# A kernel of conv, attention and experts on one core: no loops, and a rebuilt opening

## The chip, the cores and the metric

The kernel runs on one core of a Trainium2 chip. The metric is the device time in microseconds (us) of one execution. The kernel before took 2601.42 us (median of 3 runs, 2597.09 to 2603.22). One more execution was taken by the hardware profiler: 2608.5 us, with a span of 2606.6 us from its first to its last instruction.

## The reference

The input `x` has 32 images of 56 x 56 x 32 in float32. Three blocks follow one another, each with a residual:

- Group norm (a statistic for each image and channel), batch norm over all images, signs, and a 3 x 3 convolution with binarized weights.
- Layer norm, then linear attention in 16 heads of 32. Keys and queries are `elu + 1`, weighted by a cosine and a sine of the position. Key-value sums are taken over all 3136 tokens of an image. The division, the value projection and the dense projection follow.
- Layer norm, a router over 8 experts, the best two of each token, and their weighted sum.

The batch norm needs the mean and the variance of all 32 images before the first image can be binarized. So the whole of `x` is read twice: once for the statistics, once for the work.

## The kernel before

**Opening.** SyncE issues all DMAs. `x` comes in eight chunks of four images (1568 KB each) into two staging buffers `stage[0]` and `stage[1]`. TensorE transposes each image in 7 tiles (L509). VectorE takes `bn_stats` of the two PSUM banks (L861) and releases them. A chunk may be loaded into a staging buffer when TensorE has turned the chunk before it there (`stage_turned`). SyncE issues the eye matrix, five small constants (L430), chunks 0 and 1 (L435), then twenty weights and tables (L446), and only then, in a loop, chunks 2 to 7 (L450). After them it issues the loads of image 0 (L462). TensorE's and VectorE's parts of the opening are loops too. VectorE's loop covers the first 24 images. Then it waits for all 25 constants, makes the constants of the convolution (L871 to L883), the float16 halves of the weights wq, wk and we (L887 to L889) and the selector `sel16` (L890), and measures the last eight images. It then aggregates 32 images (L894), and exchanges two small matmuls with TensorE (L518, L520) for the mean and the variance.

**The value fold.** Behind that, VectorE writes one head's value weights four times side by side (L909), TensorE multiplies them with the dense weights (L524), and this is done for 16 heads with two buffers in turn. ScalarE copies the result into `p2` (L667). GpSimd raises 32 variances to the power -0.5 (L770) and then one more number (L772). VectorE makes the scale and the threshold of the binarization (L918 to L926). Then the main part begins (first instruction L539).

**Main part.** A list `ORDER`, written out by hand, gives every step of an image a time within a period of 14, for each engine. `iteration(engine, i)` sorts the steps of the images in flight. Iterations go from -3 to 34. `walk` emits iterations -3 to 2 one after the other, then 3 to 28 in a loop that has two of them in its body (13 passes, 12 jumps back on each engine), then 29 to 34 one after the other. In the loop, waits and addresses are computed from the counter by registers.

Steps that are named below: XT (L539, transposes of an image), XC (L553, a centring matmul, the first of it is the mark by which an image is timed here), K and Q (L567, L592), R and RP (L618, the spread of the denominators), PN1 (GpSimd's L778, the first of its work in the main part).

Of the kernel before, what the change touches and what calls it, by code (L numbers as in the profile page):

```python
# [9 lines left out]
ALU = mybir.AluOpType  # L10
# [7 lines left out]
TILES = 7  # L18
# [171 lines left out]
LOOP_FIRST, LOOP_LAST = 3, B - 4  # L190


# [26 lines left out]
def walk(eng, name, step):  # L219

    tables = [rounds(RING, RING_SLOTS), rounds(MISC, 1)]

    def lookup(kind, m, n, t):
        if kind not in RING and kind not in MISC:
            return None
        table = tables[kind in MISC]
        n = n // 4 if kind == "DN" else n
        slot, no, before = table[kind, m, n]
        if t is not None:
            (_, no2, before2), last = table[kind, m + 2, n], LOOP_LAST - LOOP_FIRST - 1  # L230
            slot_z, no_z, before_z = table[kind, m + last, n]
            assert no_z == no + (no2 - no) * (last // 2) and slot_z == slot
            assert before_z == (before[0], before[1] + last, before[2])
            no = t * (no2 - no) + no
        if before is not None:
            before = (before[0], Img(t, before[1]), before[2])
        return slot, no, before

    def run(i, t=None):
        for kind, m, n in iteration(name, i):  # L240
            step(kind, Img(t, m), n, lookup(kind, m, n, t))

    for i in ITERATIONS:
        if i < LOOP_FIRST:
            run(i)
    with eng.Fori(0, (LOOP_LAST + 1 - LOOP_FIRST) // 2) as t:
        run(LOOP_FIRST, t)
        run(LOOP_FIRST + 1, t)
    for i in ITERATIONS:
        if i > LOOP_LAST:  # L250
            run(i)


def build(nc, x, gamma, beta, conv_taps, conv_rows, wq, wk, wv, wd, wd_b, we, eyec, eyem, mean4, pair, dsum, sel,
          p2c, tabdc, tabnc, tabkc, firstc, validc, out):
    ctx = ExitStack()
    with ctx:
# [80 lines left out]
        wvr = xres[0:32, 0:128]  # L338
# [16 lines left out]
        consts_in = sem("consts_in")  # L355
        eye_in = sem("eye_in")
# [69 lines left out]
        def _(sp):  # L426
            sp.dma_start(eye_center[:, :], eyec).then_inc(eye_in, 16)
            for dst, src in ((mean4_sb[:, :], mean4), (views["rows"], conv_rows),
                             (small[:, 0:1], gamma), (small[:, 1:2], beta), (small[:, 2:3], wd_b)):
                sp.dma_start(dst, src).then_inc(consts_in, 16)  # L430
            x4 = x.rearrange("(q b) h w c -> q b (h w c)", b=4).rearrange("q b (p f) -> q p b f", p=PT)

            def stage_load(q, k, turned):
                wait(sp, stage_turned, turned)
                sp.dma_start(stage[k], q).then_inc(stage_in[k], 16)  # L435

            for k in range(2):
                stage_load(x4[k], k, 0)
            for dst, src in ((pair_sb[:, :], pair), (eye_mean[:, :], eyem), (dsum_sb[:, :], dsum), (views["taps"], conv_taps),
                             (views["valid"], validc), (views["wqa"], wq[0]), (wqb_s, wq[1]), (views["wka"], wk[0]),  # L440
                             (wkb_s, wk[1]), (views["wea"], we[0]), (web_s, we[1]), (wva_s, wv[0]), (wvb_s, wv[1]),
                             (wd_s, wd), (p2[:, :, :, :, :].rearrange("p a b c d -> p (a b c d)"), p2c),
                             (tabd[:, :, :].rearrange("p a b -> p (a b)"), tabdc), (tabk[:, :, :].rearrange("p a b -> p (a b)"), tabkc),
                             (first[:, :], firstc), (views["sel"], sel),
                             (tabn[:, :, :].rearrange("p a b -> p (a b)"), tabnc)):
                sp.dma_start(dst, src).then_inc(consts_in, 16)  # L446
            with sp.Fori(1, 4) as t:
                for k in range(2):
                    wait(sp, stage_turned, t * 8 + (4 * k - 4))
                    sp.dma_start(stage[k], x4[bass.ds(t * 2 + k, 1)].rearrange("q p b f -> (q p) b f"))\  # L450
                        .then_inc(stage_in[k], 16)
# [44 lines left out]
        def _(pe):  # L496
# [3 lines left out]
            def turn(t):  # L500
                for k in range(2):
                    pe.wait_ge(stage_in[k], t * 16 + 16)
                    for b in range(4):

                        wait(pe, stage_read, t * 8 + (4 * k + b - 3))
                        for j in range(TILES):
                            bank = 2 * b + (j >= 4)
                            dst = ps[:, bank, (j % 4) * PT:(j % 4 + 1) * PT]
                            mm = pe.transpose(dst, stage[k][:, b, j * 128:(j + 1) * 128], eye[0:PT, 0:PT])  # L509
                        mm.then_inc(stage_turned, 1)  # L510

            turn(0)
            with pe.Fori(1, 4) as t:
                turn(t)

            pe.wait_ge(consts_in, 16 * 25)
# [4 lines left out]

            for h in range(HEADS):
                pe.wait_ge(dve_pre, 3 + h)
                mm = pe.matmul(ps[:, 2, C * h:C * h + C], wvr[:, :] if h % 2 == 0 else xres[0:32, 128:256],  # L524
                               wd_s[:, C * h:C * h + C], start=True, stop=True)
                mm.then_inc(pe_pre, 1)

            def step(kind, m, n, rd):
# [34 lines left out]
                elif kind == "K":  # L563
                    pe.wait_ge(z_in[0], m.at(256, 256))
                    for k in range(2):
# [90 lines left out]
            pe.wait_ge(dve_pre, 22)  # L656
# [4 lines left out]
        def _(act):  # L661
            act.wait_ge(dve_pre, 19)
# [7 lines left out]
            act.wait_ge(dve_pre, 22)  # L670
# [95 lines left out]
        def _(pool):  # L766
            nc.gpsimd.memset(power[:, :], -0.5).then_inc(pool_pre, 1)
            pool.wait_ge(pool_pre, 1)
            pool.wait_ge(dve_pre, 20)
            nc.gpsimd.tensor_tensor(bw[:, 4, :], bw[:, 3, :], power[:, :], ALU.pow).then_inc(pool_pre, 1)  # L770
            pool.wait_ge(dve_pre, 21)
            nc.gpsimd.tensor_tensor(bn_inv, bn_half, power[:, 0:1], ALU.pow).then_inc(pool_pre, 1)  # L772

# [63 lines left out]
        def _(dve):  # L837
# [17 lines left out]
            def measure(t):  # L855
                for k in range(2):
                    for b in range(4):
                        img = t * 8 + (4 * k + b)
                        dve.wait_ge(stage_turned, img + 1)
                        for h in range(2):  # L860
                            last = v.bn_stats(stats[:, bass.ds(img, 1), 6 * h:6 * h + 6].rearrange("p a k -> p (a k)"),  # L861
                                              ps[:, 2 * b + h, 0:HALF[h] * PT])
                        last.then_inc(stage_read, 1)

            with dve.Fori(0, 3) as t:
                measure(t)

            dve.wait_ge(consts_in, 16 * 25)
# [12 lines left out]
            link(v.tensor_scalar(tmp, views["taps"], 0.0, 2.0, ALU.is_ge, ALU.mult))  # L881
            link(v.tensor_scalar(tmp, tmp, -1.0, None, ALU.add))
            link(v.tensor_tensor(conv_w[:, :, :].rearrange("p a b -> p (a b)"), tmp, views["valid"], ALU.mult))  # L883

            for dst, a, b, w in ((wq16, views["wqa"], wqb_s, DH), (wk16, views["wka"], wkb_s, DH),
                                 (we16, views["wea"], web_s, 264)):
                link(v.tensor_tensor(a, a, b, ALU.subtract))  # L887
                link(v.tensor_copy(dst[:, 0:w], a))
# [231 lines left out]
```

## Time and profile before

| what | value |
|---|---|
| median of 3 runs | 2601.42 us |
| profiled execution, its time | 2608.5 us |
| its span | 2606.6 us |
| TensorE matmul busy | 2302.2 us, 88% |
| VectorE busy | 2190.3 us, 84% |
| GpSimd busy | 1733.6 us, 67% |
| ScalarE busy | 1559.9 us, 60% |
| mean granted TensorE clock | 0.954 |
| first instruction of the main part | 105.4 us |

Busy time is the time in which an engine executes. The granted clock is the share of 2.4 GHz that TensorE was given; 0.50 is 1.2 GHz. The chain of waits is the work that ended last, followed back from the end. "issue" as the cause of an idle time means that the engine waited for nothing that the profile shows.

### The profile page before, as it was taken

How to read it: one execution, taken by the hardware profiler on the slowest of the kernel's cores; microseconds unless marked ns; L12 is line 12 of the kernel's file. 1: busy time of each engine (PE TensorE's matmuls, PEld its weight loads, DVE VectorE, ACT ScalarE, POOL GpSimd, SP SyncE). 2: the span in 40 equal slices, each digit the busy share in tenths (PEclk: the TensorE clock that was granted, in tenths of full speed). 3: DMA queues.
4: the chain of work that ended last, by engine and by line, in shares of the span. 5: the costliest groups of instructions: out<-in, count | busy, mean ns of one | idle time of the engine just before them, and what ended most of it. 6: DMA issues, size and time to landing. Idle time of an engine off the chain costs nothing.

```text
span 2606.6 us, 51821 instructions
## 1 busy us (share of the span) xinstructions
PE 2302.2 (88%) x15908; PEld 1110.7 (43%) x15908; DVE 2190.3 (84%) x2976; ACT 1559.9 (60%) x2757; POOL 1733.6 (67%) x1415
## 2 busy tenths in 40 slices
PE   3458999999999999999999999999999999999962
PEld 3313444444444434444443444444443444444431
DVE  3447899899898989899898989889898989999962
ACT  0046766567666666576666666666666657666620
POOL 0123477777776777777677767767676777777675
PEclk7579999999999999999999999999999999999985
DMA  8211112122221211122211111222111122211001
GB/s 249 49 28 24 33 33 38 32 42 42 42 42 33 34 31 35 36 42 41 42 34 30 34 33 39 42 42 42 31 35 31 34 38 42 41 35 32 20 19 25
DMA packets 284893, 105.84 MB, mean 41 GB/s; under 512 B 246032, under 2 KB 279680, under 8 KB 284512
## 3 DMA queue, kind: packets, MB, share of 16 engines
q1 hardware_dynamic: 284640, 102.41, 19.9%
q8 instruction: 166, 2.72, 0.5%
q14 instruction: 87, 0.71, 0.1%
HBM read 31.19 MB, written 12.85 MB: 17 GB/s over the span
## 4 chain that ended last, share of the span: by engine, by line
PE 57%; DVE 21%; issue 11%; POOL 3%; ACT 3%; DMA 2%; SPq 2%; DVEq 0%; ACTq 0%; POOLq 0%
PE ps L576 11%; PE ps L627 9%; PE ps L567 6%; PE ps L601 6%; DVE qbuf L981 6%; PE ps L618 5%; PE ps L592 4%; DVE kbuf L975 4%; PE ps L652 3%; DVE rs L998 2%; PE ps L553 2%; PE ps L646 2%; PE ps L560 2%; PE ps L640 2%; DMA qbuf<-in_x 2%
## 5 line engine op out<-in xcount | busy, mean ns | idle before, releaser
L701 ACT ACTIVATE ebuf<-ps,small 112x1024 f32<-112x1024 f32 x448 | 499.4, 1115 | 357.4 <-PE ps L567 306.4
L795 POOL TENSOR_TENSOR qbuf<-spread_r,qbuf 128x896 f32<-128x896 f32 x224 | 468.6, 2092 | 354.5 <-ACT spread_r L736 354.5
L975 DVE SCALAR_TENSOR_TENSOR kbuf<-ps,ebuf 112x1024 f32<-112x1024 f32 x448 | 544.3, 1215 | 106.6 <-ACT ebuf L701 103.0
L706 ACT ACTIVATE ebuf<-ps,small 128x896 f32<-128x896 f32 x448 | 451.8, 1009 | 206.4 <-PE ps L592 150.5
L981 DVE SCALAR_TENSOR_TENSOR qbuf<-ps,ebuf 128x896 f32<-128x896 f32 x448 | 485.5, 1084 | 15.8 <-ACT ebuf L706 14.6
L576 PE MATMUL ps<-kbuf,xcs 112*64 112x512 f32 x1792 | 482.9, 617 | 6.8 <-DVE kbuf L975 6.2
L627 PE MATMUL ps<-qbuf,gmat 128*64 128x224 f32 x3584 | 387.2, 358 | 2.9 <-DVE pbuf L1009 2.9
L778 POOL TENSOR_TENSOR rstd<-varr,power 112x28 f32<-112x28 f32 x64 | 307.3, 4802 | 80.9 <-DVE varr L960 77.4
L567 PE MATMUL ps<-wk,z 128*112 128x512 f16 x896 | 287.7, 404 | 61.0 <-DVE qbuf L981 33.6
L824 POOL TENSOR_TENSOR prod<-prod 112x512 f32<-112x512 f32 x224 | 285.5, 1275 | 54.7 <-DVE prod L1065 54.7
L627 PEld LDWEIGHTS ps<-qbuf,gmat 128*64 128x64 f32 x3584 | 240.2, 136 | 155.7 <-issue 81.9
L1065 DVE TENSOR_TENSOR prod<-ps,gate 112x1024 f32<-112x1024 f32 x224 | 272.8, 1220 | 34.8 <-PE ps L652 19.2
L618 PE MATMUL ps<-rs,sel 128*128 128x448 f16 x896 | 248.0, 360 | 53.7 <-issue 36.1
L1003 DVE TENSOR_TENSOR qbuf<-ps,qbuf 128x896 f32<-128x896 f32 x224 | 243.2, 1086 | 33.9 <-PE ps L618 31.4
L592 PE MATMUL ps<-z,wq 128*128 128x448 f16 x896 | 245.8, 356 | 14.4 <-ACT spread_r L736 6.2
L736 ACT ACTIVATE spread_r<-ps 128x896 f32<-128x896 f32 x224 | 204.6, 913 | 64.3 <-PE ps L618 35.7
L601 PE MATMUL ps<-qbuf,dmat 128*32 128x448 f32 x1792 | 237.1, 569 | 1.1 <-DVE pbuf L1009 1.1
L567 PEld LDWEIGHTS ps<-wk,z 128*112 128x112 f16 x896 | 90.3, 131 | 267.4 <-issue 99.7
L827 POOL TENSOR_TENSOR prod<-prod 112x256 f32<-112x256 f32 x224 | 163.4, 729 | 17.6
L652 PE MATMUL ps<-we,z 128*112 128x256 f16 x896 | 148.0, 291 | 22.3 <-DVE prod L1065 10.2
L618 PEld LDWEIGHTS ps<-rs,sel 128*128 128x128 f16 x896 | 63.0, 101 | 233.1 <-issue 138.5
L576 PEld LDWEIGHTS ps<-kbuf,xcs 112*64 112x64 f32 x1792 | 96.3, 136 | 148.9 <-issue 96.2
(131 smaller groups left out, 3090.7 us busy)
## 6 DMA issues: line engine op xcount, KB each, us to landing
z<-zhl SPq DMA_DIRECT2D x1024, 49.0 KB, 1.9
qbuf<-in_x SPq DMA_DIRECT2D x8, 1568.0 KB, 12.2
xt<-in_x SPq DMA_DIRECT2D x256, 49.0 KB
out<-ffn SPq DMA_DIRECT2D x256, 49.0 KB
shifted<-nat SPq DMA_DIRECT2D x128, 52.6 KB, 5.1
qbuf<-in_sel SPq DMA_DIRECT2D x1, 1024.0 KB, 12.0
tabn<-in_tabnc SPq DMA_DIRECT2D x1, 784.0 KB, 14.1
p<-in_p2c SPq DMA_DIRECT2D x1, 528.0 KB, 10.5
```

The lines of the kernel that those rows point to most:

```text
L567: mm = pe.matmul(o[0:PT, k, :], z1[:, m.par, s % G, s // G, :], wk16[:, :], start=True, stop=True)
L576: mm = pe.matmul(kt_bank[64 * k:64 * k + 64, :], xcs[:, 2 * n + k, :, :].rearrange("p a c -> p (a c)"), kbuf[:, n % 2, DH * k:DH * k + DH] ...
L592: mm = pe.matmul(o[:, k, 0:G * PT].rearrange("p (g t) -> p g t", g=G), wq16[:, 128 * (k0 + k):128 * (k0 + k) + 128], z1[:, m.par, :, j, :] ...
L601: mm = pe.matmul(o[32 * j:32 * j + 32, 0:HW4], dmat[:, m.par, c, :, :].rearrange("p a h -> p (a h)"), qbuf[:, c, 4 * h + j, :], start=(c = ...
L618: mm = pe.matmul(o[:, k, 0:HW4], sel16[:, 128 * a:128 * a + 128], rs[:, j // 4, :], start=True, stop=True)
L627: mm = pe.matmul(o[64 * v:64 * v + 64, 0:2 * PT].rearrange("p (a t) -> p a t", a=2), gmat[:, m.par, c, :, :].rearrange("p a o -> p (a o)") ...
L701: act.activation(ebuf[0:PT, 0, :].rearrange("p (a b) -> p a b", a=2), o[0:PT, :, :], ACT.Exp, bias=minus_one[0:PT, :]).then_inc(kexp_made, 1)
L706: act.activation(ebuf[:, 1, 0:2 * G * PT].rearrange("p (a b) -> p a b", a=2), o[:, :, 0:G * PT], ACT.Exp, bias=minus_one).then_inc(qexp_ma ...
L778: nc.gpsimd.tensor_tensor(rstd[ln][:, :], varr[ln][:, :], power[0:PT, 0:SLOTS], ALU.pow)\
L795: nc.gpsimd.tensor_tensor(qbuf[:, 2:4, n, :], spread_r[:, :, :], qbuf[:, 2:4, n, :], ALU.mult)\
L975: v.scalar_tensor_tensor(kbuf[:, n % 2, :].rearrange("p (a b) -> p a b", a=2), o[0:PT, :, :], 1.0, ebuf[0:PT, 0, :].rearrange("p (a b) -> ...
L981: v.scalar_tensor_tensor(qbuf[:, k0:k0 + 2, j, :], o[:, :, 0:G * PT], 1.0, ebuf[:, 1, 0:2 * G * PT].rearrange("p (a b) -> p a b", a=2), AL ...
```

## The change

- All loops are written out: the six-chunk loop of SyncE, TensorE's and VectorE's loops of the opening, and the loop of 13 passes in `walk`, on all engines.
- SyncE issues the eye, chunks 0 and 1, five constants, chunks 2 to 7, then eleven weights (`weights_in`) and nine tables (`tables_in`), then the loads of image 0.
- VectorE makes the constants that need only `rows`, gamma and beta first, then measures all chunks, and aggregates eight images after every two chunks. It passes the variance to GpSimd before it touches any weight.
- The value fold has one replication for all 16 heads, into `kbuf`, and 16 matmuls behind it with one signal at the end.
- The constants of the convolution that need `taps` stand behind the replication.
- The halves of wk, wq and we and the selector are made by GpSimd, behind its second power. TensorE waits for them (`weights_made`) ahead of the first K of each image.
- TensorE waits for ScalarE's `p2`, for VectorE's thresholds and for the tables before the main part.

```diff
     for i in ITERATIONS:
-        if i < LOOP_FIRST:
-            run(i)
-    with eng.Fori(0, (LOOP_LAST + 1 - LOOP_FIRST) // 2) as t:
-        run(LOOP_FIRST, t)
-        run(LOOP_FIRST + 1, t)
-    for i in ITERATIONS:
-        if i > LOOP_LAST:
-            run(i)
+        run(i)
...
             sp.dma_start(eye_center[:, :], eyec).then_inc(eye_in, 16)
+            for k in range(2):
+                sp.dma_start(stage[k], x4[k]).then_inc(stage_in[k], 16)
...
+            for q in range(2, 8):
+                sp.wait_ge(stage_turned, 4 * q - 4)
+                sp.dma_start(stage[q % 2], x4[q]).then_inc(stage_in[q % 2], 16)
+            for dst, src in ((views["taps"], conv_taps), (views["valid"], validc), (wva_s, wv[0]), (wvb_s, wv[1]), (wd_s, wd),
+                             (views["wqa"], wq[0]), (wqb_s, wq[1]), (views["wka"], wk[0]), (wkb_s, wk[1]),
+                             (views["wea"], we[0]), (web_s, we[1])):
+                sp.dma_start(dst, src).then_inc(weights_in, 16)
...
-            pe.wait_ge(consts_in, 16 * 25)
+            pe.wait_ge(consts_in, 16 * 5)
...
+            pe.wait_ge(weights_in, 16 * 11)
+            pe.wait_ge(dve_pre, 4)
             for h in range(HEADS):
-                pe.wait_ge(dve_pre, 3 + h)
-                mm = pe.matmul(ps[:, 2, C * h:C * h + C], wvr[:, :] if h % 2 == 0 else xres[0:32, 128:256],
-                               wd_s[:, C * h:C * h + C], start=True, stop=True)
-                mm.then_inc(pe_pre, 1)
+                mm = pe.matmul(ps[:, 2, C * h:C * h + C], wvr[:, 128 * h:128 * h + 128], wd_s[:, C * h:C * h + C], start=True, stop=True)
+            mm.then_inc(pe_pre, 1)
...
-            act.wait_ge(dve_pre, 19)
+            act.wait_ge(tables_in, 16 * 9)
+            act.wait_ge(pe_pre, 3)
...
+            pool.wait_ge(weights_in, 16 * 11)
+            pool.wait_ge(tables_in, 16 * 9)
+            done = 3
+            for dst, a, b, w in ((wk16, views["wka"], wkb_s, DH), (wq16, views["wqa"], wqb_s, DH),
+                                 (we16, views["wea"], web_s, 264)):
+                nc.gpsimd.tensor_tensor(a, a, b, ALU.subtract).then_inc(pool_pre, 1)
+                pool.wait_ge(pool_pre, done + 1)
+                nc.gpsimd.tensor_copy(dst[:, 0:w], a).then_inc(pool_pre, 1)
+                pool.wait_ge(pool_pre, done + 2)
+                nc.gpsimd.tensor_tensor(dst[64:128, 0:w], a[64:128], dst[64:128, 0:w], ALU.subtract).then_inc(pool_pre, 1)
+                done += 3
+                pool.wait_ge(pool_pre, done)
+            nc.gpsimd.tensor_copy(sel16[:, :], views["sel"]).then_inc(weights_made, 1)
...
-            dve.wait_ge(consts_in, 16 * 25)
+            dve.wait_ge(consts_in, 16 * 5)
...
+            for t in range(4):
+                for b in range(8):
+                    img = 8 * t + b
+                    dve.wait_ge(stage_turned, img + 1)
+                    for h in range(2):
+                        last = v.bn_stats(stats[:, img, 6 * h:6 * h + 6], ps[:, 2 * (b % 4) + h, 0:HALF[h] * PT])
+                    last.then_inc(stage_read, 1)
+                dve.wait_ge(stage_read, 8 * t + 8)
+                for img in range(8 * t, 8 * t + 8):
+                    last = v.bn_aggr(mv[:, img, :], stats[:, img, :])
+                last.then_inc(aggregated, 1)
...
+            dve.wait_ge(pe_pre, 2)
+            link(v.tensor_scalar(bw[:, 3, :], ps[:, 1, 0:B], GN_EPS, None, ALU.add))
+            v.tensor_copy(bw[:, 7, :], ps[:, 1, 0:B]).then_inc(dve_pre, 1)
+
+            dve.wait_ge(weights_in, 16 * 11)
             link(v.tensor_tensor(wva_s, wva_s, wvb_s, ALU.subtract))
-            for h in range(HEADS):
-                if h >= 2:
-                    dve.wait_ge(pe_pre, 2 + h - 1)
-                o = 128 * (h % 2)
-                v.tensor_copy(xres[0:32, o:o + 128].rearrange("p (k a) -> p k a", k=4),
-                              wva_s[:, C * h:C * h + C].unsqueeze(1).to_broadcast([32, 4, C])).then_inc(dve_pre, 1)
+            v.tensor_copy(wvr.rearrange("p (h k a) -> p h k a", h=HEADS, k=4),
+                          wva_s.rearrange("p (h a) -> p h a", h=HEADS).unsqueeze(2).to_broadcast([32, HEADS, 4, C])).then_inc(dve_pre, 1)
```

## Rows read from the trace of the kernel before

**Rows 1.** Windows by stretch: interval; sum, busy time of engines; clock, DMA share, GB/s.

```profile
519.35:590.77 71.42, 69.05 (x491) 32.98 (x490) 66.32 (x89) 48.58 (x87) 53.96 (x45) 1.00 0.21 38
442.06:519.35 77.29, 70.93 (x492) 33.11 (x491) 66.81 (x89) 48.56 (x87) 53.99 (x45) 0.98 0.19 36
1033.10:1111.63 78.53, 72.42 (x492) 33.62 (x491) 66.78 (x89) 48.57 (x87) 53.96 (x45) 0.96 0.17 35
2225.71:2297.11 71.40, 69.04 (x491) 32.98 (x490) 66.56 (x89) 48.70 (x87) 54.04 (x45) 1.00 0.20 38
442.06:2154.27 1712.21, 1612.49 (x11250) 761.44 (x11248) 1530.88 (x2025) 1117.18 (x1979) 1241.16 (x1013) 0.99 0.20 37
```

**Rows 2.** Waits: engine, line, releaser; total us, times, longest.

```profile
PE ps L618 <- issue: 36.1, 12, 3.2
```

**Rows 3.** Windows of 4 us around one of those twelve waits.

```profile
1096.00:1100.00 4.00, 1.30 (x4) 0.57 (x4) 1.39 (x2) 0.00 (x0) 3.83 (x3) 0.75 0.01 4
1100.00:1104.00 4.00, 4.00 (x17) 1.04 (x16) 1.96 (x2) 1.11 (x1) 0.44 (x1) 0.50 0.00 0
```

**Rows 4.** DMA queues, instruction fetches (packets, MB, share): from 442.06, then from 519.35.

```profile
q8 instruction: 7, 0.11, 0.7%
...
q8 instruction: 4, 0.07, 0.4%
```

**Rows 5.** Timeline of the opening, TensorE and SyncE: start, us, instruction, idle before.

```profile
3.59 0.96 SPq L435 DMA_DIRECT2D qbuf<-in_x  x2
...
12.46 4.57 PE L509 MATMUL ps<-eye_center,qbuf 112*128 112x112 f32 x28 [12.46 <-DMA qbuf<-in_x]
...
39.19 4.86 PE L509 MATMUL ps<-eye_center,qbuf 112*128 112x112 f32 x28 [17.75 <-DMA qbuf<-in_x]
44.32 2.90 PE L509 MATMUL ps<-eye_center,qbuf 112*128 112x112 f32 x28 [0.26 <-DMA qbuf<-in_x]
...
69.36 5.13 PE L509 MATMUL ps<-eye_center,qbuf 112*128 112x112 f32 x28 [6.68 <-DMA qbuf<-in_x]
76.95 4.58 PE L509 MATMUL ps<-eye_center,qbuf 112*128 112x112 f32 x28 [2.46 <-DVE dcs L861]
```

**Rows 6.** Windows of the opening.

```profile
18.00:33.00 15.00, 2.90 (x28) 2.69 (x28) 4.38 (x10) 0.00 (x0) 0.00 (x0) 0.77 1.05 360
46.00:57.00 11.00, 4.15 (x29) 3.94 (x28) 4.34 (x10) 0.00 (x0) 0.00 (x0) 0.69 1.02 277
...
88.00:97.00 9.00, 8.19 (x34) 7.89 (x34) 4.32 (x21) 0.38 (x1) 0.00 (x0) 0.50 0.00 0
```

**Rows 7.** Timeline, VectorE's chain of constants, its first and tenth instruction.

```profile
64.61 0.29 DVE L871 TENSOR_SCALAR xres<-qbuf 128x288 f32<-128x288 f32 x1
...
67.67 0.15 DVE L880 TENSOR_SCALAR small<-small 128x1 f32<-128x1 f32 x1
```

**Rows 8.** Chain of waits from the last chunk to the main part: start, us, what.

```profile
83.55 2.45 DVE den L894 x32
...
87.87 0.60 DVE t L904
...
88.76 7.64 PE ps L524 x32
...
97.24 5.45 POOL den L770
...
105.40 0.63 PE ps L539 x2
```

**Rows 9.** Timeline of the opening: ScalarE's copy into p2, VectorE's cast of the selector.

```profile
74.59 1.23 DVE L890 CAST sel<-qbuf 128x2048 f16<-128x2048 f32 x1
...
96.62 2.39 ACT L667 ACTIVATE p<-ps 32x512 f32<-32x512 f32 x4 [94.58 <-DVE small L912]
```

**Rows 10.** GpSimd: its common operation of 512 elements (groups by shape), its first work in the main part (timeline).

```profile
L824 POOL TENSOR_TENSOR prod<-prod 112x512 f32<-112x512 f32 x224 | 285.5, 1275 | 54.7 <-DVE prod L1065 54.7
...
128.42 4.80 POOL L778 TENSOR_TENSOR rstd<-varr,power 112x28 f32<-112x28 f32 x1 [24.23 <-DVE varr L960]
```

More of the change, by code:

```diff
@@ L188 @@
 }
-LOOP_FIRST, LOOP_LAST = 3, B - 4
 def iteration(engine, i):
@@ L228, in lookup @@
         slot, no, before = table[kind, m, n]
[L229 to L234, printed above, removed]
         if before is not None:
@@ L355, in build @@
         consts_in = sem("consts_in")
+        weights_in = sem("weights_in")
+        tables_in = sem("tables_in")
+        weights_made = sem("weights_made")
+        aggregated = sem("aggregated")
         eye_in = sem("eye_in")
@@ L430, in _ @@
                 sp.dma_start(dst, src).then_inc(consts_in, 16)
[L431 to L451, printed above, removed]
+            for q in range(2, 8):
[5 more added lines that the diff above has]
+                sp.dma_start(dst, src).then_inc(weights_in, 16)
@@ new lines, in _ @@
+            for dst, src in ((p2[:, :, :, :, :].rearrange("p a b c d -> p (a b c d)"), p2c),
+                             (tabk[:, :, :].rearrange("p a b -> p (a b)"), tabkc), (dsum_sb[:, :], dsum),
+                             (tabd[:, :, :].rearrange("p a b -> p (a b)"), tabdc), (views["sel"], sel),
+                             (tabn[:, :, :].rearrange("p a b -> p (a b)"), tabnc), (pair_sb[:, :], pair),
+                             (eye_mean[:, :], eyem), (first[:, :], firstc)):
+                sp.dma_start(dst, src).then_inc(tables_in, 16)
@@ L499, in _ @@
             pe.wait_ge(eye_in, 16)
[L500 to L514, printed above, removed]
-            pe.wait_ge(consts_in, 16 * 25)
+            for q in range(8):
+                pe.wait_ge(stage_in[q % 2], 16 * (q // 2) + 16)
+                for b in range(4):
+                    if 4 * q + b >= 4:
+                        pe.wait_ge(stage_read, 4 * q + b - 3)
+                    for j in range(TILES):
+                        dst = ps[:, 2 * b + (j >= 4), (j % 4) * PT:(j % 4 + 1) * PT]
+                        mm = pe.transpose(dst, stage[q % 2][:, b, j * 128:(j + 1) * 128], eye[0:PT, 0:PT])
+                    mm.then_inc(stage_turned, 1)
+            pe.wait_ge(consts_in, 16 * 5)
             pe.wait_ge(dve_pre, 1)
@@ L564, in step @@
                     pe.wait_ge(z_in[0], m.at(256, 256))
+                    if n == 0:
+                        pe.wait_ge(weights_made, 1)
                     for k in range(2):
@@ L654, in step @@
                     mm.then_inc(ring_full, 1)
-            pe.wait_ge(dve_pre, 22)
+            pe.wait_ge(act_pre, 1)
+            pe.wait_ge(dve_pre, 6)
+            pe.wait_ge(tables_in, 16 * 9)
             walk(pe, "tensor", step)
@@ L669, in _ @@
             last.then_inc(act_pre, 1)
-            act.wait_ge(dve_pre, 22)
+            act.wait_ge(dve_pre, 6)
             def step(kind, m, n, rd):
@@ L853, in _ @@
                 link(v.memset(xn[ln][:, :, C - 1:C], 1.0))
[L855 to L866, printed above, removed]
-            dve.wait_ge(consts_in, 16 * 25)
+            dve.wait_ge(consts_in, 16 * 5)
             rows, rows2, tmp = views["rows"], views["rows2"], views["tmp"]
@@ L880, in _ @@
             link(v.tensor_scalar(conv_scale2, conv_scale, 2.0, None, ALU.mult))
[L881 to L888, printed above, removed]
-                link(v.tensor_tensor(dst[64:128, 0:w], a[64:128], dst[64:128, 0:w], ALU.subtract))
-            link(v.tensor_copy(sel16[:, :], views["sel"]))
-            measure(3)
-            dve.wait_ge(stage_read, B)
-            for b in range(B):
-                last = v.bn_aggr(mv[:, b, :], stats[:, b, :])
-            link(last)
+            for t in range(4):
[9 more added lines that the diff above has]
+                last.then_inc(aggregated, 1)
+            dve.wait_ge(aggregated, 4)
             v.tensor_copy(bw[:, 0, :], mv[:, :, 0]).then_inc(dve_pre, 1)
```

18 lines of the change are left out of this document (9 added, 9 removed).

## The prediction

> **What bounds the kernel now.** I first cut the span by image: the windows between the XC steps of successive images. A short interval is 71.42 us with 69.05 us of matmuls at a full clock [rows 1]: TensorE is busy 97% of it, so the main part is TensorE's. But every second interval of the looped stretch is long, 77.29 and 78.53 us in the two shown, for the same 491 or 492 matmuls [rows 1]. The list of waits says what ends the extra idle time: nothing. R or RP on TensorE sat idle before "issue" 12 times, 36.1 us together, 3.2 at most [rows 2]. The loop has 13 passes, so 12 jumps back, and the long intervals lie 147 to 150 us apart, one per pass. The windows around one such stall show a second part: in the next 4 us the granted clock is 0.50, that is 1.2 GHz, after 0.75 [rows 3]. TensorE had stood still before the clock fell. And in a long interval one queue fetched instructions 7 times, in a short one 4 times [rows 4]. At the two ends of the main part, where iterations are written out, the interval is 71.40 [rows 1].
>
> Then the opening, by its timeline. Up to 105.40 us nothing of the main part runs [rows 8]. Chunk 2 of x is turned from 39.19 on and chunk 0 from 12.46 [rows 5]: between them lie the twenty weights and tables, which were issued ahead of chunk 2.
>
> **Part 1: the loop of the main part.** The stretch from 442.06 to 2154.27 holds 12 long and 11 short intervals. 1712.21 - 23 x 71.42 = 69.6 us is what the long ones have too much [rows 1]. Of that 36.1 is the stall [rows 2], 1612.49 - 23 x 69.05 = 24.3 is matmuls that took longer at the lower clock [rows 1], and 9 is waits that follow. Written out, all of it goes: **-69.6 us**. What is late next is TensorE itself at 71.4 per image, as the written-out interval shows. That the waits are constants now gives nothing more, since a short looped interval and a written-out one differ by 0.02 us. Bounds: from -69.6 to, if only the stalls go and the clock still falls somewhere, -36.1. I take the first, since an interval that is really written out stands in the rows.
>
> Here a rule of the Trainium skill bears on it. In these rows a jump back costs 3.0 us of stall (36.1 / 12) [rows 2]. "Advanced Engine Details and Errata", section Control Flow Timing, gives a compare-and-branch about 108 ns. By that rule the loop would cost 1.3 us in all and the long intervals would have another cause. "Runtime: NRT & Kernel Launch", section Instruction fetch mechanics, speaks of the other side: code is fetched ahead in sequence only, and a taken branch to code that isn't held waits for a DMA. The three additional fetches of a long interval [rows 4] agree with that page.
>
> **Part 2: when the last chunk of x lands.** Chunk 0 was issued at 3.59 and turned from 12.46 on [rows 5]. Now it is issued straight behind the eye, at about 1.2: turned from 10.1 on. From then on two buffers turn. Between chunks 2 and 6, so over two pairs, 69.36 - 39.19 = 30.2 us passed [rows 5], 15.1 a pair. Three pairs behind chunk 0 is chunk 6 at 55.4, and chunk 7 comes 5.1 (chunks 2 to 3, rows 5) to 6 us later, 61. The weights queued behind it share its transfer: 0.5. So **61.5**, where the kernel before turned chunk 7 from 76.95 on.
>
> VectorE is now late at first: five constants lie behind chunk 1 in the queue (about 16.5), then ten small instructions run from 64.61 to 67.8, 3.2 us [rows 7]. It reads chunk 0 from about 20 on, and chunk 3 is issued some 6 us late. Chunk 2 then has the queue for itself and chunk 4 isn't later than in the pattern of 15.1, so I put the delay at 0 with up to 5. Lower end: 12.85 MB (eight chunks of 1568 KB) at the 277 GB/s of rows 6 without a pause are 46.4 us, so 52. Upper end: 66.
>
> **Part 3: from that landing to the main part.** Turning chunk 7 takes 4.9 at the low clock [rows 5], plus 0.3 to begin and 1.1 for the last two statistics: 6.3. The last 8 of 32 aggregations: 0.6 instead of 2.45 [rows 8]. From there to the second signal 1.9 (86.0 to 87.87), and 1.1 for the matmul and two small instructions to the variance: 9.9. Now three branches run beside each other.
>
> - Power: 5.45 on GpSimd [rows 8], then 2.7 as between 102.7 and 105.40: 18.1.
> - Fold: subtraction 0.7, one replication of 2048 elements 1.3 (as the cast of 2048, rows 9), 32 matmuls 7.7, ScalarE's copy 2.4 [rows 9] and two hand-overs 0.3: 9.9 + 12.4 = 22.3.
> - Tables: the weights and tables are 5.0 MB by their widths in the code; at 360 GB/s [rows 6] some 14 behind the last chunk, then ScalarE's copy: 17. SyncE issues them, then the loads of image 0, which land about 15.5 behind.
>
> The fold ends last. Before, VectorE's copies and TensorE took turns, but TensorE had no idle time in these 7.64 us [rows 8], with the clock at 0.50 [rows 6], so fewer hand-overs don't shorten it. It is now hidden behind the power only in part. The main part begins at 61.5 + 22.3 = 83.8 instead of 105.4: **-21.6 us**. Bounds: 52 + 18.1 = 70 (clock full, fold short), and 66 + 24 = 90. The replication alone lies between 0.8 and 2.2, the latter at a subtraction's pace.
>
> **Part 4: the halves on GpSimd.** Off VectorE go nine operations and a cast, 6.4 us that stood ahead of the last chunk's statistics; part 2 has that gain already. On GpSimd 512 elements of two operands take 1.28 [rows 10]: six of them 7.7, three of 264 about 2.2, the cast of 2048 between 1.2 and 5.1; I take 4. Some 14 us, from about 5.5 us before the main part begins. GpSimd's first work there came 128.42 - 105.40 = 23.0 us after its beginning [rows 10]. The work is done by 8.5, so 14 us are left, and the first K comes later still. **0**, between 0 and +10 if the casts are several times slower. Behind TensorE's wait for them stand all its later steps, but it is passed before its first use. If GpSimd's work were slow enough, XC's layer norm would be late by the same amount.
>
> **Sum.** 2606.6 - 69.6 - 21.6 = 2515.4 of span, and 1.9 around it: 2517.3 by the profiled execution, which was 7.1 above the median of the runs shown. If these 7.1 are slower jumps back (the two shown exceed a short one by 5.9 and 7.1), they go with the loop and 2517 stays; if they are spread, 2510. I take **2514 us**.
>
> **The rivals.**
>
> - The opening gives little or nothing: the fold at 24 us, the late VectorE and slower tables leave the main part at 98 to 105. For it: bytes and fold are unchanged. Against: 13 us of constants no longer stand between chunks of x. About 2536.
> - The opening gives more: x without a pause, the fold at the full clock, beginning at 74: about 2504.
> - The long intervals aren't the loop's. The body holds two images, and buffers alternate by parity, so an alternation could lie in the schedule. For it: they alternate strictly. Against: the written-out ones don't. Only the opening is gained: 2514 + 69.6 = 2584. The rule on Control Flow Timing of the Trainium skill, cited above, would end here.
> - Slower: written-out code stalls for instructions. It has 4 fetches per image [rows 4], some 130 in the run; each that isn't ready costs TensorE 3.0 us and the clock behind it. From 91 / 3.0 = 30 stalls on the kernel is slower; at all 130 it takes about 2904. Against: the interval of 71.40 had 4 fetches too and no stall. What speaks for it is that only two to three such intervals exist at each end.
>
> **How the numbers follow.** Likeliest, with 2514: 0.70. Opening little: 0.12. Opening more: 0.10. Alternation without the loop: 0.05. Slower: 0.03. The likeliest case and the second and third fill 2500 to 2534, which leaves out the last two and the tails. Changes below 0.2%, 5 us, can't be told from none; both gains would have to fail. Faster 0.96, same 0.01, slower 0.03.
>
> **What would show it.** All intervals between XC steps from image 5 on at 71.4, no "issue" waits of 2 us or more on R and RP, granted clock 1.00 throughout, and mean clock up from 0.954. The first L539 at about 84. Chunk 7's transposes from about 61. The last thing ahead of the main part is ScalarE's copy, not VectorE's thresholds. GpSimd's ten operations end before the first variance of the main part. I am wrong if intervals stay long, if they grow evenly above 71.4, or if the tables or GpSimd's weights hold up the first steps.

## The result

The changed kernel takes 2511.42 us (median of 4 runs, 2509.60 to 2512.61), the kernel before 2600.06 in the same session (2597.09 to 2603.22). The ratio is 0.9658, 95% interval 0.9642 to 0.9675: 88.6 us less. Forecast were 2514 us. The profiled execution took 2511.5 us, with a span of 2509.7: 96.9 less span than before. It lies at the median, unlike the profiled execution of before, so at least part of the 7.1 us there went too.

The page of the changed kernel: span, busy time, granted clock in tenths, instruction fetches (packets, MB, share).

```profile
span 2509.7 us, 45423 instructions
...
PE 2271.0 (90%) x15908; PEld 1106.9 (44%) x15908; DVE 2175.7 (87%) x2949; ACT 1560.4 (62%) x2757; POOL 1745.9 (70%) x1425
...
PEclk8579999999999999999999999999999999999985
...
q8 instruction: 131, 2.15, 0.4%
```

Its windows by image, from XC to XC, with the columns of [rows 1]; the second row is the stretch of 12 long and 11 short intervals of before:

```profile
491.94:563.12 71.18, 68.81 (x492) 32.98 (x490) 66.21 (x89) 48.59 (x87) 54.05 (x45) 1.00 0.21 38
...
420.74:2058.33 1637.59, 1583.16 (x11249) 758.74 (x11248) 1523.24 (x2025) 1117.75 (x1979) 1243.16 (x1013) 1.00 0.20 38
```

The same 23 intervals took 1712.21 us [rows 1] and take 1637.59: 74.6 less, with 29.3 us less of busy TensorE for the same matmuls, and a clock of 1.00. No wait of R or RP for "issue" is left in the list of waits. In the page, q8 fetched 131 blocks instead of 166: in the trace of before, a long and a short interval together fetched 11 blocks there [rows 4], and two written-out images fetch about 8.

The timeline of its opening, from the last chunk of x on (start, us, instruction, idle before):

```profile
61.87 5.22 PE L490 MATMUL ps<-eye_center,qbuf 112*128 112x112 f32 x28 [4.25 <-DMA qbuf<-in_x]
...
71.86 5.74 POOL L752 TENSOR_TENSOR den<-den,power 128x32 f32<-128x32 f32 x1 [71.00 <-DVE den L887]
72.33 1.22 DVE L891 COPY kbuf<-t 32x2048 f32<-32x2048 f32 x1
...
73.69 7.00 PE L502 MATMUL ps<-t1b,kbuf 32*128 32x32 f32 x32 [2.44 <-DVE kbuf L891]
...
79.14 1.26 POOL L761 TENSOR_TENSOR qbuf<-qbuf,ebuf 128x512 f32<-128x512 f32 x1
79.21 1.21 DVE L903 TENSOR_TENSOR small<-small 128x1 f32<-128x1 f32 x1 [0.68 <-POOL small L754]
...
80.78 1.28 ACT L649 ACT_TABLE_LOAD   x1 [80.78 <-PE ps L502]
...
82.07 2.39 ACT L649 ACTIVATE p<-ps 32x512 f32<-32x512 f32 x4
82.42 0.15 DVE L907 COPY small<-small 128x1 f32<-128x1 f32 x1
...
84.51 1.01 PE L516 MATMUL ps<-eye_center,xt 112*128 112x112 f32 x4 [3.83 <-ACT p L649]
...
87.71 1.89 POOL L768 CAST sel<-qbuf 128x2048 f16<-128x2048 f32 x1
...
107.82 4.80 POOL L775 TENSOR_TENSOR rstd<-varr,power 112x28 f32<-112x28 f32 x1 [18.22 <-DVE varr L940]
```

The last chunk is turned from 61.87 on (before 76.95 [rows 5]), and the main part begins at 84.51 instead of 105.40: 20.9 us. Both ends scatter: in five other executions with this opening (e2 to e5 and e9 below) the last chunk comes at 61.48 to 63.52 and the main part begins at 84.05 to 86.44. Two others with the opening of before (e1, e10) begin it at 102.94 and 103.03, so some 2 us of the 20.9 belong to the one execution of before. Read the last wait of TensorE: it ends by ScalarE's copy, whose own first row is a table load of 1.28 us. GpSimd's ten operations are over at 89.6, 18.2 us before its next work.

### The profile page after: what moved, and what is told of

It is laid out like the page before. It is cut to its first block, busy times and chain, and to the rows that moved or that the text cites. A ratio compares the mean times of both kernels' runs of the same rounds, so it can differ in the third digit from the quotient of the medians.

```text
span 2509.7 us, 45423 instructions
## 1 busy us (share of the span) xinstructions
PE 2271.0 (90%) x15908; PEld 1106.9 (44%) x15908; DVE 2175.7 (87%) x2949; ACT 1560.4 (62%) x2757; POOL 1745.9 (70%) x1425
## 3 DMA queue, kind: packets, MB, share of 16 engines
q8 instruction: 131, 2.15, 0.4%
## 4 chain that ended last, share of the span: by engine, by line
PE 60%; DVE 23%; issue 9%; POOL 3%; ACT 2%; DMA 2%; SPq 1%; POOLq 0%; DVEq 0%; ACTq 0%
PE ps L555 12%; PE ps L606 10%; PE ps L546 7%; DVE qbuf L961 6%; PE ps L580 6%; PE ps L597 5%; PE ps L571 4%; DVE kbuf L955 4%; PE ps L631 3%; DVE prod L1045 2%; DVE rs L978 2%; DVE qbuf L983 2%; PE ps L530 2%; PE ps L537 2%; PE ps L625 2%
## 5 line engine op out<-in xcount | busy, mean ns | idle before, releaser
L775 POOL TENSOR_TENSOR rstd<-varr,power 112x28 f32<-112x28 f32 x64 | 307.3, 4802 | 74.9 <-DVE varr L940 71.4
L597 PE MATMUL ps<-rs,sel 128*128 128x448 f16 x896 | 241.0, 356 | 17.4 <-DVE kbuf L955 14.8
L580 PE MATMUL ps<-qbuf,dmat 128*32 128x448 f32 x1792 | 225.9, 549 | 1.1 <-DVE pbuf L989 1.1
L546 PEld LDWEIGHTS ps<-wk,z 128*112 128x112 f16 x896 | 90.1, 129 | 255.7 <-issue 96.9
```

The lines of the kernel that those rows point to most:

```text
L546: mm = pe.matmul(o[0:PT, k, :], z1[:, m.par, s % G, s // G, :], wk16[:, :], start=True, stop=True)
L580: mm = pe.matmul(o[32 * j:32 * j + 32, 0:HW4], dmat[:, m.par, c, :, :].rearrange("p a h -> p (a h)"), qbuf[:, c, 4 * h + j, :], start=(c = ...
L597: mm = pe.matmul(o[:, k, 0:HW4], sel16[:, 128 * a:128 * a + 128], rs[:, j // 4, :], start=True, stop=True)
```

## The experiments

Each run was measured beside executions of the kernel before. Their median was 2600.06 us beside the changed kernel, 2604.44 beside e1 to e4, 2597.09 beside e5 to e8, 2598.92 beside e9, v1 and v2, and 2610.70 beside e10. Differences between runs of different groups are uncertain by some us. For the loop there is a firmer measure, the 23 image intervals of one trace, which the result gave as 1712.21 and 1637.59 us.

### The loop alone, and the loop put back

e1: the kernel before, with only the loop of `walk` written out.

```diff
     for i in ITERATIONS:
-        if i < LOOP_FIRST:
-            run(i)
-    with eng.Fori(0, (LOOP_LAST + 1 - LOOP_FIRST) // 2) as t:
-        run(LOOP_FIRST, t)
-        run(LOOP_FIRST + 1, t)
-    for i in ITERATIONS:
-        if i > LOOP_LAST:
-            run(i)
+        run(i)
```

> The kernel before, with the loop of the main part alone written out; its opening stays. Theory (the jumps back cost some 5.8 us each, and every looped image 0.2 more): 75 us go, so a span near 2531 and a time near 2526 to 2533, all intervals between images at 71.2, main part from 105.4 on. Rival (the long intervals alternate with the image's parity and the buffers): the time stays near 2600. Rival (the opening and the loop depend on each other, so that the gain needs both): clearly less than 75 goes.

Measured: 2530.62 us, ratio 0.9719 (0.9688 to 0.9751), span 2527.8. A window between two XC, the one that had been long:

```profile
438.58:509.79 71.21, 68.85 (x492) 32.99 (x490) 66.23 (x89) 48.60 (x87) 54.09 (x45) 1.00 0.21 38
```

The kernel before took 2604.44 beside it, so 73.8 us went, 75 were expected. So the long intervals are the loop's, and the gains need not each other: the new opening then takes off some 19 us more (2530.62 to 2511.42).

e2: the changed kernel, with that loop put back.

```diff
+LOOP_FIRST, LOOP_LAST, BODY = 3, 28, 2
...
     for i in ITERATIONS:
-        run(i)
+        if i < LOOP_FIRST:
+            run(i)
+    with eng.Fori(0, (LOOP_LAST + 1 - LOOP_FIRST) // BODY) as t:
+        for i in range(BODY):
+            run(LOOP_FIRST + i, t)
+    for i in ITERATIONS:
+        if i > LOOP_LAST:
+            run(i)
```

> The changed kernel, with the loop of 13 passes put back on all engines; its opening stays new. Theory: 2511 + 75 = 2586 us, 12 long intervals of 76 to 79 us, main part from 84.5 on. Rival (the alternation is not the loop's): 2511.

Measured: 2608.11 us, ratio to the kernel before 1.0016 (0.9999 to 1.0033). The direction is as expected, the size is not: under the new opening the loop costs 96.7 us, not 75. The traces agree: the 23 intervals take 1731.75 us here, 94.2 more than written out, where the old loop's took 74.6 more. Its windows, one long and one short, then its list of waits:

```profile
422.05:501.07 79.02, 72.01 (x491) 33.41 (x490) 66.76 (x89) 48.51 (x87) 53.96 (x45) 0.96 0.19 35
501.07:572.72 71.65, 68.94 (x492) 32.99 (x491) 66.17 (x89) 48.54 (x87) 54.00 (x45) 1.00 0.20 38
```

```profile
PE ps L618 <- issue: 35.7, 12, 3.2
...
DVE kbuf L976 <- issue: 18.3, 7, 2.8
```

TensorE's stall is the old one (36.1 before [rows 2]). VectorE stands still ahead of the same instruction at all 12 jumps, for 2.5 to 2.8 us (2.6 on average); the list puts 7 of them down to issue and 5 to ScalarE. In the trace of before VectorE stands still there too, 12 times for 1.5 to 1.8 us (1.6 on average), all put down to ScalarE, so they don't appear as issue. One of them:

```profile
1093.32 1.23 DVE L975 SCALAR_TENSOR_TENSOR kbuf<-ps,ebuf 112x1024 f32<-112x1024 f32 x1 [1.61 <-ACT ebuf L701]
```

So the stall of VectorE isn't new, it is longer. Short looped intervals are 71.65, written-out ones 71.2.

### Whose jump it is

e3 keeps the loop on TensorE alone, e4 on the four others (`if name == "tensor"` and its opposite around the loop of e2).

> The changed kernel, with the loop on TensorE alone; the other engines are written out. Theory (TensorE bounds the main part, so only its own jump matters): near the time with all loops, 2575 to 2586. Rival (the stall of TensorE is the aftermath of jumps on VectorE, ScalarE or SyncE, which hold up its operands): near 2511 to 2525.

> The changed kernel, with the loop on VectorE, ScalarE, GpSimd and SyncE, and TensorE written out. Theory (only TensorE's own jump matters): 2511 to 2518. Rival (jumps of the others hold up TensorE): 2560 or more. If both this and the run with TensorE's loop are long, each engine's jump costs on its own.

Measured: e3 2559.91, e4 2547.65 us (2 runs each). Windows of e3 and of e4, a long and a short interval each:

```profile
420.01:493.46 73.45, 68.91 (x492) 32.99 (x490) 66.33 (x89) 48.60 (x87) 54.13 (x45) 1.00 0.21 37
493.46:564.68 71.22, 68.86 (x492) 32.98 (x490) 66.24 (x89) 48.59 (x87) 54.12 (x45) 1.00 0.20 38
```

```profile
422.31:495.88 73.57, 69.48 (x492) 32.83 (x491) 66.61 (x89) 48.56 (x87) 54.04 (x45) 1.00 0.21 37
495.88:567.55 71.67, 68.94 (x491) 33.00 (x490) 66.19 (x89) 48.58 (x87) 54.05 (x45) 1.00 0.19 38
```

The long interval shown of e3 is its shortest; the other eleven are 73.6 to 75.6. In e4 all twelve are 73.5 to 73.7. The same 23 intervals, each kernel in its own trace:

| kernel | looped engines | 23 intervals, us | above the changed kernel |
|---|---|---|---|
| changed kernel | none | 1637.59 | |
| e1 (old opening) | none | 1638.08 | 0.5 |
| e3 | TensorE | 1684.02 | 46.4 |
| e4 | the four others | 1671.03 | 33.4 |
| e2 | all five | 1731.75 | 94.2 |
| before (old opening) | all five | 1712.21 | 74.6 |

Both pure theories fall. The loop on TensorE costs 48.5 us in the runs' times, that on the four others 36.2, together 84.7 of the 96.7: both reach the path, and both at once cost a little more. Which of the four others counts wasn't tried one by one. The short intervals separate a second cost. With TensorE alone in a loop they are 71.22, as when written out. With the others looped they are 71.67, some 0.45 us longer. So of e4's 36.2 us the twelve jumps make about 23 (12 x 1.9), the rest comes with each looped image. That this rest is TensorE waiting for engines whose waits and addresses come from registers is an inference: no run changes the registers alone.

The pages also say whose code each fetch queue brings. q8 has 154 blocks in e2 and e3 and 131 in e4, as in the changed kernel: it is TensorE's. q14 stays at 92 in e3, as in the changed kernel, and has 147 in e4: it serves the others. Here are q14's lines of before, of the changed kernel and of e2:

```profile
q14 instruction: 87, 0.71, 0.1%
...
q14 instruction: 92, 0.75, 0.1%
...
q14 instruction: 147, 1.20, 0.2%
```

So under the new opening the others' loop fetches 60 blocks more than the same loop did before, five more in each pass, and their jumps are dearer.

e5: a loop of 6 passes over 4 images (`LOOP_LAST, BODY = 26, 4`).

> The changed kernel with a loop of 6 passes over 4 images on all engines (images of iterations 3 to 26): 5 jumps back instead of 12, and 24 looped iterations instead of 26. Theory (what is lost is 7.1 us per jump, as between the long and short intervals of the run with the loop back, and 0.47 us per looped iteration): 5 x 7.1 + 24 x 0.47 = 47 us above the changed kernel, 2558; every fourth interval long. Rival (computed waits cost, the jumps are incidental): 24/26 of the 97 us of the loop of 2, so 2600.

Measured: 2556.09 us, where 2558 was expected. Four intervals in a row:

```profile
421.47:492.87 71.40, 69.03 (x491) 32.98 (x490) 66.19 (x89) 48.59 (x87) 53.99 (x45) 1.00 0.21 38
492.87:564.28 71.41, 69.04 (x491) 33.00 (x490) 66.65 (x89) 48.66 (x87) 54.00 (x45) 1.00 0.21 38
564.28:643.69 79.41, 72.35 (x491) 33.60 (x490) 66.75 (x89) 48.56 (x87) 54.13 (x45) 0.96 0.18 35
643.69:715.33 71.64, 68.93 (x491) 32.99 (x490) 66.17 (x89) 48.58 (x87) 54.01 (x45) 1.00 0.19 38
```

Every fourth is long, none of the others. The cost goes by jumps: 5 of 7.5 to 8.0 us. The rest splits as well: of the looped intervals only the first and those behind a long one are 71.65, the others are 71.4. So 0.2 us come with each looped image, and 0.25 more only where the loop has just begun or jumped. In e2 and e4 every short interval stands behind a jump. From 2608 to 2556, 5 jumps instead of 12 win back 52 of the 96.7 us.

### Why the same loop costs 97 or 75

e9: e2 with 128 small memsets at VectorE's start, so that its code lies elsewhere.

```diff
...
+            for k in range(128):
+                v.memset(spread_r[:, 0, k:k + 1], 0.0)
...
```

> The run with the loop put back, with 128 small memsets more on VectorE at its start, in the time in which it waits for x: its code is moved by 128 instructions, nothing else changes. It is for the difference that is open: the same loop costs 97 us in the changed kernel and 75 in the kernel before, with VectorE standing still for 2.6 us on issue at each jump in the one and not in the other. Theory (what a jump back costs depends on where target and end lie in the blocks in which code is fetched): the VectorE stall and the long intervals change, by 1 us or more for each of 12, and the time leaves 2608 by 12 us or more, most likely down. Rival (the difference lies in the instructions themselves): 2608 stays, within 3.

Measured: 2608.21 us, and VectorE's row at the same jump:

```profile
484.28 1.22 DVE L978 SCALAR_TENSOR_TENSOR kbuf<-ps,ebuf 112x1024 f32<-112x1024 f32 x1 [2.64 <-issue]
```

Nothing changed: VectorE stands still for 2.6 to 2.8 us at all 12 jumps, the long intervals are 77.8 to 78.8. But this is a weak test of the theory. The page of e9 has one fetch more on q14 than that of e2, 148 blocks against 147, of 8 KB each:

```profile
q14 instruction: 148, 1.21, 0.2%
```

So the 128 instructions fill about one block. If they fill exactly one, every later instruction keeps its place within its block, and the theory about places in a block stands untested. A shift by half as much would test it.

e10: the kernel before, with only its opening's loops written out.

```diff
...
-            with pe.Fori(1, 4) as t:
+            for t in range(1, 4):
                 turn(t)
...
-            with dve.Fori(0, 3) as t:
+            for t in range(3):
                 measure(t)
```

> The kernel before with the loops of its opening alone written out, on SyncE, TensorE and VectorE; order of loads, fold and the loop of the main part stay. It is for what is left open: the same loop of the main part cost 97 us under the new opening and 75 under the old. Theory (the new opening's longer written-out code moves or enlarges the program, and this alone makes the jumps dearer): the long intervals grow to 78 to 79 and short ones to 71.65, 2615 to 2622. Rival (the difference comes from elsewhere in the new opening, such as the order of the loads or the place of the weights): 2598 to 2603, intervals as before.

Measured: 2634.74 us, ratio 1.0094 (1.0073 to 1.0115): slower than before. The kernel before took 2610.70 beside it, so the loss is 24.0 us; expected were 15 to 22. The 23 intervals take 1739.74 us, 27.5 more than before. A long and a short interval, then VectorE's waits:

```profile
439.00:518.96 79.96, 71.72 (x491) 33.17 (x490) 66.79 (x89) 48.55 (x87) 54.02 (x45) 0.96 0.19 35
518.96:590.39 71.43, 69.06 (x491) 32.98 (x490) 66.31 (x89) 48.59 (x87) 54.01 (x45) 1.00 0.21 38
```

```profile
DVE kbuf L973 <- issue: 43.1, 12, 3.8
```

So the code ahead of the loop is enough, without new loads, fold or weights: with the opening written out, VectorE stands still 3.6 us on average at every jump of a loop whose body is the same, where it was 1.6 before. Twelve times the difference is 23.5 us, about the loss. q14 goes from 87 blocks to 147, as in e2, so the dearer jumps go together with more fetching by the engines beside TensorE. What in the code ahead decides it (its length, its own loops, the place in a block) stays open. The short intervals stay at 71.43 here and are 71.65 in e2; that difference is open too.

### The opening

e6: the changed kernel with the lines that load chunks 2 to 7 moved behind the weights and tables.

> The changed kernel with the weights and tables issued ahead of chunk 2 of x again. Theory (they held up x by their transfer time): chunk 2 some 13 us later, the main part from 98 on, 2525. Rival (the bytes are the same, and tables at the end hold up the main part as much): 2511. Rival (the opening's gain is in the chain behind x): 2511 to 2514.

Measured: 2520.57 us, ratio to before 0.9707 (0.9680 to 0.9735), so 9.2 us above the changed kernel. Its timeline:

```profile
74.13 2.90 PE L490 MATMUL ps<-eye_center,qbuf 112*128 112x112 f32 x28 [0.99 <-DMA qbuf<-in_x]
...
95.50 1.01 PE L516 MATMUL ps<-eye_center,xt 112*128 112x112 f32 x4 [3.82 <-ACT p L649]
```

In these two traces the order of loads is worth 12.3 us of the last chunk's landing and 11.0 of the beginning of the main part; by the runs' times it is 9.2, about half of the opening's gain. Of the other 9.9 us between this trace and that of before, 2.8 lie ahead of the last chunk (74.13 against 76.95) and 7.1 behind it (21.4 us to the main part against 28.5).

e7: the fold in 16 turns again, with a semaphore each way.

```diff
...
+            for h in range(HEADS):
+                if h >= 2:
+                    dve.wait_ge(fold_read, h - 1)
+                o = 128 * (h % 2)
+                v.tensor_copy(wvr[:, o:o + 128].rearrange("p (k a) -> p k a", k=4),
+                              wva_s[:, C * h:C * h + C].unsqueeze(1).to_broadcast([32, 4, C])).then_inc(fold_made, 1)
...
```

> The changed kernel with the replication in 16 turns and two buffers again, behind the variance's signal to GpSimd. Theory (TensorE's 32 matmuls take 7 us either way; what one replication frees is VectorE, which then makes conv_w and the thresholds): the last copy 0.5 us later, VectorE busy up to 81, the thresholds at 87: main part 2 to 3 us later, 2514. Rival (hand-overs cost, and the fold gets longer by 16 of them): 5 us or more. Rival: no change, 2511.

Measured: 2510.91 us, no difference to 2511.42 (0.9672, 0.9645 to 0.9700, against 0.9658). Its timeline:

```profile
60.95 5.35 PE L492 MATMUL ps<-eye_center,qbuf 112*128 112x112 f32 x28 [5.18 <-DMA qbuf<-in_x]
...
71.89 7.59 PE L505 MATMUL ps<-t1b,kbuf 32*128 32x32 f32 x32 [1.44 <-DVE kbuf L898]
...
80.86 2.39 ACT L652 ACTIVATE p<-ps 32x512 f32<-32x512 f32 x4
...
85.14 0.15 DVE L915 COPY small<-small 128x1 f32<-128x1 f32 x1
85.40 0.98 PE L519 MATMUL ps<-eye_center,xt 112*128 112x112 f32 x4 [5.91 <-issue]
```

From the last chunk on, 24.45 us instead of 22.64, and ScalarE's copy ends 0.3 us earlier, not later: the mechanism is as expected (VectorE's thresholds are late), the price of 1.8 us is under the 2 to 3 of the sum, and the last chunk landed 0.9 earlier in this execution. In the runs' time it can't be seen. Here GpSimd's halves are not free: beside them VectorE's three threshold instructions take 2.2 us longer than in e8 below, and in this run they end last.

e8: the halves and the selector by VectorE again, ahead of `dve.wait_ge(pool_pre, 2)`, the selector at the end.

> The changed kernel with the halves of the weights and the selector made by VectorE again, in the shadow of GpSimd's power and ahead of its first step of the main part. Theory (ScalarE's copy of the fold ends last, and GpSimd's weights only saved time off the path; they even made VectorE's threshold instructions longer, 1.21 us instead of 0.16 for the first): VectorE's thresholds 0 to 1 us later than in the changed kernel, main part from 84.5 on, 2511 to 2512. Rival (moving 6.4 us off VectorE is worth its time): 2515 to 2518.

Measured: 2512.99 us (0.9675, 0.9647 to 0.9702): no difference. In its timeline GpSimd is quiet, and the first threshold instruction is short again:

```profile
64.91 5.41 PE L490 MATMUL ps<-eye_center,qbuf 112*128 112x112 f32 x28 [4.73 <-DMA qbuf<-in_x]
...
84.92 0.16 DVE L894 TENSOR_TENSOR small<-small 128x1 f32<-128x1 f32 x1 [0.68 <-POOL small L754]
...
87.75 1.01 PE L516 MATMUL ps<-eye_center,xt 112*128 112x112 f32 x4 [3.82 <-ACT p L649]
```

From the last chunk to the main part 22.84 us, against 22.64. Moving the halves to GpSimd gained nothing once they stand off the path. That the last chunk was turned from 60.95 in one execution, 61.87 and 64.91 in others of the same order of loads, shows how much the opening scatters.

### A version that beats both

v1: 16 chunks of two images in four buffers, constants behind the first chunk, image 0's loads ahead of the tables, tables awaited at XC, ScalarE's table loaded at the start, GpSimd's weights behind the thresholds.

```diff
+            for q in range(4, 16):
+                sp.wait_ge(stage_turned, 2 * q - 6)
+                sp.dma_start(stage[q % 4], x2[q]).then_inc(stage_in[q % 4], 16)
...
+            act.activation(spread_r[:, 0, 1:2], spread_r[:, 0, 0:1], ACT.Copy)
```

> The changed kernel with x in 16 chunks of two images and four staging buffers in the same space, the five constants behind the first chunk, image 0's loads ahead of the tables, the tables waited for at XC only, ScalarE's table loaded at the start, and GpSimd's weights behind the thresholds. Theory (two large chunks in turn leave the DMA queue idle, and behind the last chunk the fold's chain ends last): last chunk lands near 54.5, main part from about 74 on instead of 84.5, 2500. Rival (x is bound by its transfer rate with 3584-byte pieces, and smaller chunks gain nothing): last chunk at 60, main part from 79 on, 2506.

v2: v1 with the fold spread over the transposes.

> The run before with the value fold done in the time in which x is loaded: its weights behind the first four chunks, one head per image from image 12 on, into columns of PSUM that the transposes leave free. Theory: behind the last chunk the power's branch ends last, 3 us less than the fold's: main part near 71, 2497. Rival (the fold's matmuls slow the transposes, and the last chunk comes later by as much): no difference to the run before, 2500.

Measured: v1 2500.99 us, ratio 0.9623 (0.9604 to 0.9642); v2 2505.11, 0.9632 (0.9613 to 0.9651). v1 is the fastest here, 10.4 us below the changed kernel by the medians. It changes several things at once, and no run separates them. Its timeline, then a window of the changed kernel and one of v1 over the loading of x, then one of v1 and one of v2 from 30 us on, then v2's start of the main part:

```profile
56.41 1.56 PE L500 MATMUL ps<-eye_center,qbuf 112*128 112x112 f32 x14 [1.60 <-DMA qbuf<-in_x]
...
74.56 1.01 PE L525 MATMUL ps<-eye_center,xt 112*128 112x112 f32 x4 [2.54 <-ACT p L661]
```

```profile
8.00:60.00 52.00, 27.70 (x196) 26.48 (x196) 32.40 (x90) 0.00 (x0) 0.00 (x0) 0.83 0.86 220
```

```profile
8.00:55.00 47.00, 35.42 (x206) 31.04 (x204) 34.30 (x92) 0.00 (x0) 0.00 (x0) 0.71 1.04 255
```

```profile
30.00:50.00 20.00, 17.25 (x84) 15.16 (x84) 13.45 (x41) 0.00 (x0) 0.00 (x0) 0.50 1.03 255
```

```profile
30.00:58.00 28.00, 28.00 (x124) 23.22 (x122) 15.50 (x43) 0.00 (x0) 0.00 (x0) 0.50 0.95 232
```

```profile
78.79 0.98 PE L527 MATMUL ps<-eye_center,xt 112*128 112x112 f32 x4 [8.91 <-issue]
```

v1 keeps the DMA engines at work (share 1.04 instead of 0.86) and starts 10.0 us earlier, as summed. In v2 the theory falls in part: at a granted clock of 0.50 TensorE is busy 86% of the stretch in v1 already, and the fold's matmuls make it 100%. TensorE then turns its last 35 tiles from 60.04 on without waiting for a chunk, so it is late and not the loads (236 GB/s from 30 to 50 us, instead of 255). It is done 7.4 us later than v1, at 65.4. The power's branch does end last, and from the variance to the main part it takes 8.5 us instead of 11.5, the 3 us expected. The main part begins 4.2 us later than in v1.

## Why the prediction was right

- **Loop.** The 69.6 us of the long intervals went, as did the stall, the low clock behind it and the three fetches. The sum missed 5 us: "a short looped interval and a written-out one differ by 0.02 us" was wrong. The interval read for it, 2225.71 to 2297.11 [rows 1], is iteration 28, mostly the loop's last: the stalls lie some 63 us behind the XC mark (1096 in the interval from 1033.10 on), so the loop ends that late in it. A written-out interval stood in the same trace, ahead of the loop:

```profile
299.41:370.61 71.20, 68.84 (x492) 32.98 (x491) 66.28 (x89) 48.59 (x87) 51.94 (x44) 1.00 0.18 33
```

It is 71.2, a short looped one 71.42: 0.2 us in each of some 25 images. By e3 and e4 it comes with the looped engines beside TensorE. The two bounds of this step had -69.6 as their larger end; it measured -74.6.
- **Rule on branches.** A jump of all engines makes its interval 4 to 8 us longer (before, e2, e5). The rule of the Trainium skill in "Runtime: NRT & Kernel Launch", Instruction fetch mechanics, that a taken branch waits for its code, agrees in kind; it gives no figure. The 108 ns of "Advanced Engine Details and Errata", Control Flow Timing, in the Trainium skill isn't what a jump of this size costs: 36.1 us of stall for 12 jumps [rows 2]. That the stall is the wait for code is inferred: the fetches rise with it (rows 4; q14 in e2 and e10), and no run changes the fetching alone.
- **Whose stall it is.** I put the whole cost on TensorE's row, and e3 and e4 share it out between TensorE and the others. Written out on all engines the sum was the same; on TensorE alone it would have been wrong.
- **Last chunk**: 61.5 forecast, 61.87 measured. Part of this closeness is luck: five other executions with this opening lie at 61.48 to 63.52, and the steps were off both ways. Chunk 0 was turned from 10.57 on (10.1 forecast), two pairs of chunks took 31.3 us with VectorE late (30.2), the third 12.9 (15.1), and chunk 7 came 7.2 behind chunk 6 (5.6 to 6.5). e6 shows the loads' order as the cause of 12.3 of the 15.1 us. The other 2.8 weren't tried apart; before, chunk 7 waited 2.46 us for VectorE [rows 5], and now it waits for its DMA.
- **From there to the main part**: 22.3 forecast, 22.64 measured, by errors that cancel. The variance came after 9.84 (9.9 forecast) and the fold took 7.0 (7.7), but ScalarE's table load of 1.28 us was missed. In the timeline of before it stood at 0.76 us, while the engine had nothing to do, and now it comes behind the waits. A wait stood ahead of ScalarE's first work before too, for one semaphore; now two stand there. That the second one moves the load fits the runs (all with two waits have it late, e1 and e10 with one at 0.74 and 0.75), but no run tries it alone. An activation of one element ahead of the waits, as in v1, puts it at 0.73.
- **GpSimd's halves**: 14 us forecast, 10.5 measured, off the path both ways (e8). Not foreseen: beside them VectorE's three threshold instructions took 2.2 us longer. That, too, was hidden by the fold.
- **Sum**: the profiled execution was 5.7 us below its sum of 2515.4, nearly all of it the 0.2 us per image. The 2514 took the middle between 2517 and 2510, which made up for half of this miss by chance.

## What to carry to other kernels

A loop whose body is two images of this kernel cost a stall on TensorE and on VectorE at each jump, plus the matmuls that followed at the lower clock; look for regular long intervals, and compare with an interval that is really written out. The list of waits can put such a stall down to another engine, as it did for VectorE here, so compare the idle time at the same place of two traces as well. Fewer, longer passes buy it back in proportion to the jumps. Behind a global statistic, order loads so that nothing unneeded lies ahead of the last chunk, and add up every branch behind it, with the first-use costs that a moved wait drags along.

## What the hardware showed

- Writing out loops ahead of a loop made that loop's jumps dearer: VectorE's stall at each went from 1.6 to 3.6 us, q14's fetches from 87 to 147, and the kernel took 24 us more (e10). Half a change can be slower than none.
- With GpSimd subtracting two SBUF operands of 512 elements beside it, a VectorE instruction of 128 x 1 took 1.21 us (changed kernel, e6, e7); alone 0.16 (e8).
- Fetches of instructions come in blocks of 16 KB for TensorE (q8, 2.15 MB in 131) and 8 KB for the others (q14, 0.75 MB in 92).
- TensorE stayed at a granted clock of 0.50 for 28 us in which the trace has it busy throughout with small float32 transposes and matmuls (v2).
